# Router logits on GpSimd and VectorE instead of TensorE, in a fused attention and mixture-of-experts kernel

## The reference

```python
x = x + tanh(g_xattn[0]) * cross_attention0(ctx, layernorm(x))   # 8 heads of 64
x = x + tanh(g_ffn[0]) * experts0(layernorm(x))                  # 8 experts, top 2, capacity 40 per batch
x = x + tanh(g_xattn[1]) * linear_attention1(layernorm(x), ctx)
x = x + tanh(g_ffn[1]) * experts1(layernorm(x))

def experts0(x):                        # the part that routes
    probs = softmax(x @ Wr + br)        # Wr is 256 x 8
    topk_p, topk_e = top_k(probs, 2)
    pos = ...                           # how many earlier rows of the batch chose the same expert
    keep = pos < cap
    slot = (topk_e * B + b) * cap + min(pos, cap - 1)
    # rows go to their slots, each expert's two products run over its slots, answers are gathered back
```

## Time and profile before

| | |
|---|---|
| time, median of 3 runs (range) | 2261.21 us (2253.23 to 2261.25) |
| the profiled execution's own time | 2261.54 us |
| its span, first to last instruction | 2259.8 us |
| mean granted TensorE clock | 0.992 of full speed |
| TensorE busy | 2198.2 us (97%) |
| VectorE busy | 1615.2 us (71%) |
| ScalarE busy | 1292.9 us (57%) |
| GpSimd busy | 642.3 us (28%) |

### The profile page before, as it was taken

One profiled execution on the slowest core, in us unless ns is written; L12 is line 12 of the kernel. 1 busy time (PEld: TensorE's weight loads), 2 busy tenths in 40 slices (PEclk: granted clock), 3 DMA queues, 4 the chain that ended last, 5 costly groups with the idle time before them and its releaser, 6 DMA issues. The chain is left out here.

```text
span 2259.8 us, 49398 instructions
## 1 busy us (share of the span) xinstructions
PE 2198.2 (97%) x15486; PEld 1871.1 (83%) x15486; DVE 1615.2 (71%) x5729; ACT 1292.9 (57%) x3251; POOL 642.3 (28%) x1162
## 2 busy tenths in 40 slices
PE   9999999999999999999999999999989999999997
PEld 6777777777777777777689999999978888888886
DVE  5667677677677676777665555555579999999986
ACT  6676776776766767767533343343245555555553
POOL 1123222232232222322320000000255555555541
PEclk9999999999999999999989999999999999999999
DMA  5431111111111111111142222221222222222210
GB/s 195 136 102 45 54 44 47 53 45 47 53 36 53 44 46 54 45 47 38 40 142 72 80 85 84 67 85 47 82 59 65 64 64 63 64 68 64 64 38 19
DMA packets 136226, 146.70 MB, mean 65 GB/s; under 512 B 23090, under 2 KB 122665, under 8 KB 135840
## 3 DMA queue, kind: packets, MB, share of 16 engines
q1 hardware_dynamic: 122825, 122.13, 17.3%
q0 software_dynamic: 12288, 21.21, 3.5%
q10 hardware_dynamic: 855, 0.19, 0.1%
HBM read 101.04 MB, written 54.79 MB: 69 GB/s over the span
## 5 line engine op out<-in xcount | busy, mean ns | idle before, releaser
L735 ACT ACTIVATE a_prob<-a_prob,a_nmax 128x376 f32<-128x376 f32 x512 | 309.8, 607 | 143.8 <-DVE a_nmax L881 143.8
L881 DVE CUSTOM_DVE_ANT_0 a_prob<-a_score,a_mask_row 128x376 f32<-128x376 f32 x512 | 270.4, 543 | 92.3 <-PE a_score L1157 84.6
L1472 ACT ACTIVATE e_hidden<-e_first,keep_b 128x256 f32<-128x256 f32 x320 | 134.4, 472 | 283.0 <-PE e_first L80 282.4
L80 PE MATMUL e_second<-e_w,e_hidden 128*128 128x256 f32 x1920 | 239.5, 284 | 0.0
L80 PEld LDWEIGHTS e_second<-e_w,e_hidden 128*128 128x128 f32 x1920 | 232.6, 192 | 0.0
L1166 PE MATMUL a_turned<-keep_ident,a_prob 128*128 128x128 f32 (+1 forms) x1536 | 216.7, 277 | 1.1 <-DVE a_probT L901 0.7
L1166 PEld LDWEIGHTS a_turned<-keep_ident,a_prob 128*128 128x128 f32 (+1 forms) x1536 | 173.5, 142 | 41.0 <-issue 26.8
L743 ACT ACTIVATE a_probT<-a_turned 128x384 f32<-128x384 f32 x256 | 125.8, 492 | 127.6 <-PE a_turned L1166 127.6
L901 DVE COPY a_probT<-a_turned 128x384 f32<-128x384 f32 x256 | 141.1, 551 | 78.4 <-PE a_turned L1166 75.4
L1157 PE MATMUL a_score<-a_kT,a_qT 64*128 64x376 f32 x1024 | 196.4, 501 | 0.6
L177 POOL TENSOR_SCALAR r_var<-r_mv 128x2 f32<-128x2 f32 x64 | 12.3, 192 | 569.8 <-issue 502.4
(11 more groups left out here) (238 smaller groups left out, 5180.9 us busy)
## 6 DMA issues: line engine op xcount, KB each, us to landing
a_share<-shares SPq DMA_DIRECT2D x256, 64.0 KB, 2.6
w_in<-W SPq DMA_DIRECT2D x32, 512.0 KB, 4.2
slots<-a_zeros SPq DMA_DIRECT2D x8, 1280.0 KB, 8.6
keep_rows<-slots SPq DMA_DIRECT2D x40, 256.0 KB, 4.1
answers<-e_y SPq DMA_DIRECT2D x40, 256.0 KB, 2.2
a_xn<-x SPq DMA_DIRECT2D x32, 256.0 KB, 3.2
a_xr<-x SPq DMA_DIRECT2D x32, 256.0 KB, 3.3
shares<-a_rden_rows SPq DMA_DIRECT2D x512, 0.5 KB
```

Source lines behind the costliest of these rows:

```text
L80: last = nc.tensor.matmul(out, stationary(a, t), moving(b, t), start=start and n == 0, stop=stop and n == len(todo) - 1)
L735: nc.scalar.activation(prob[:, u % 4, a], prob[:, u % 4, a], ACT.Exp, bias=nmax[:, u % 4, a:a + 1], scale=-1.0, accum_out=den[:, u % 4, a: ...
L881: nc.vector.tensor_tensor_reduce(prob[:, u % 4, a], score[SCORE_AT[u][a]][:, 0:NKV], mask_row[:, p], -1.0, 3.0e38, ALU.add, ALU.min, nmax[ ...
L1472: nc.scalar.activation(hidden[:, 2 * j + i], first[:, j, i * CH:(i + 1) * CH], ACT.Relu, bias=b1[:, 2 * j + i, bass.ds(e, 1)]).then_inc(re ...
```

## The change

For batches 0 to 30 the router's logits no longer go through TensorE. The 256 x 8 weights are loaded once more, spread over all 128 partitions (`wr_rows`, in the space of `b2`, row by row, so that the weights of one expert lie 32 bytes apart). GpSimd multiplies the two 256-wide rows of `x2h` of each partition with the weights of expert e, for e from 0 to 7 (`weigh`, 128x512 elements each, into four rotating buffers: two in the second half of `w2_in`, `rT`, and the new `a_weighed`). VectorE sums each product over its 256 columns (`logit_part`), then adds the bias (`logits_sum`). Seven of the eight sums stand at the end of step b+3, the eighth, the bias and the shift at the beginning of step b+4, the choice behind them. `router_exp` moves to that step too.

`router_count` moves down half a step, to where `router_turn` was, and `counts_in` and `place` on VectorE with it. Both halves of `dispatch` are issued in step b+5: the first behind `norm1`, the second behind `norm2` of batch b+2. The waits that kept the banks in order are replaced by ones that fit.

As `w2_in` and `b2` are now in use until the last product, the load of the second half of the first expert's W2 and that of `b2` move from step 4 to step 34. Batch 31 in `experts` keeps the way through TensorE.

```diff
+    wr_rows = keep["b2"][:].rearrange("p e d -> p (e d)").rearrange("p (d e) -> p d e", e=E0)
+    w2_rows = keep["w2_in"][:].rearrange("p k d -> p (k d)")[:, KH * D // 2:].rearrange("p (n k d) -> p n k d", k=QT, d=D)
+    weighed = [w2_rows[:, 0], w2_rows[:, 1], rT[:].rearrange("p k (i d) -> p (k i) d", d=D)]   # a_weighed is appended
...
+    def weigh(eng, b, p, e):
+        if e == 0:
+            eng.wait_ge(x2h_ok, QT * (b + 1))
+            if b == 0:
+                eng.wait_ge(small_in, 16 * N_SMALL)
+        at_least(eng, part_ok, E0 * b + e + 1 - len(weighed))
+        nc.gpsimd.tensor_tensor(weighed[e % len(weighed)], x2h[:, p],
+                                wr_rows[:, :, e].unsqueeze(1).to_broadcast([P, QT, D]), ALU.mult).then_inc(weighed_ok, 1)
+    def logit_part(eng, b, e):
+        eng.wait_ge(weighed_ok, E0 * b + e + 1)
+        nc.vector.reduce_sum(lgr[:, :, e], weighed[e % len(weighed)], AX.X).then_inc(part_ok, 1)
+    def logits_sum(eng, b):
+        eng.wait_ge(part_ok, E0 * (b + 1))
+        nc.vector.tensor_tensor(lg[:], lgr[:], br[:].unsqueeze(1).to_broadcast([P, QT, E0]), ALU.add).then_inc(soft, 1)
...
+                     (r["wr_rows"], t["Wr0"].partition_broadcast(P))]        # one more small load
...
     GpSimd, step s
                 if here(s - 3):
                     norm1(eng, s - 3)
                 if routed(s - 5):
-                    dispatch(eng, s - 5, q, range(QT, QT * 2))
+                    dispatch(eng, s - 5, q, range(QT))
                 if live(s):
                     norm0(s)
                 if here(s - 3):
                     norm2(eng, s - 3)
-                if routed(s - 4):
-                    dispatch(eng, s - 4, p, range(QT))
+                if routed(s - 5):
+                    dispatch(eng, s - 5, q, range(QT, QT * 2))
                 if live(s - 2):
                     residual(s - 2, p)
+                if here(s - 3):
+                    for e in range(E0):
+                        weigh(eng, s - 3, q, e)
...
     ScalarE: router_in(s - 3) goes out, router_exp(s - 3) becomes router_exp(s - 4) behind exps(s - 2, 5, 1)
...
     VectorE, step s, in its new order (unchanged calls in short)
                 attended(s-3, 3); turned_out(s-2, 1, 1)
+                logit_part(eng, s - 4, 7)
                 row_max(s-2, 5, 0); att_low(s-3, 3)
+                logits_sum(eng, s - 4)
                 row_max(s-2, 5, 1)
+                logits_shift(eng, s - 4)
                 mask_line(s-1); over_sum(s-2, 1); kvin_low(s-1, 0)
                 choose 0 to 7 follow, one at a time, up to row_max(s-2, 7, 1)   # before: choose 7 in front of turned_out(s-2, 2, 1)
                 out_norm(s-3); stat(s); turned_out(s-2, 4, 1); x1_stat(s-3)
                 row_max(s-1, 0, 0) ... turned_out(s-2, 6, 1)                    # before: place 0 to 4 in here
+                counts_in(s-4); row_max(s-1, 2, 0); place 0; row_max(s-1, 2, 1); place 1
                 attended(s-2, 2)
+                logit_part 0; place 2
                 turned_out(s-2, 7, 1)
+                logit_part 1; place 3
                 row_max(s-1, 3, 0)
+                logit_part 2; place 4
                 att_low(s-2, 2)
+                logit_part 3
                 row_max(s-1, 3, 1)
+                logit_part 4
                 over_sum(s-1, 0); turned_out(s-1, 0, 1)
+                logit_part 5
                 row_max(s-1, 4, 0)
+                logit_part 6
                 row_max(s-1, 4, 1)
...
     TensorE, step s
-                if routed(s - 4):
-                    eng.wait_ge(v_ok, 3 * (s - 1))
-                    router_count(eng, s - 4, bank_b)                             # between turn_prob 2 and scores 6
...
-                if here(s - 3):
+                if routed(s - 4):
                     if s == B + 1:
                         eng.wait_ge(att_ok, KI * (s - 2) + 1)
                     else:
                         eng.wait_ge(v_ok, 3 * (s - 1) + 1)
-                    router_turn(eng, s - 3, q, bank_b)                           # between turn_prob 6 and scores 2
+                    router_count(eng, s - 4, bank_b)
...
-                    router_logits(eng, s - 3, bank_a)                            # behind times_v 2
...
     SyncE, step B + 2
+                    eng.wait_ge(part_ok, E0 * (B - 1))
+                    load_w2(1)
+                    eng.wait_ge(weighed_ok, E0 * (B - 1))
+                    eng.dma_start(keep["b2"][:], t["b2"].partition_broadcast(P)).then_inc(keep["biases_in"], 16)
```

More of the change, by code:

```diff
@@ L546, in load_w1, with load_w2 @@
                     eng.dma_start(stage_kv[:, n], t["W1"][0, n * P:(n + 1) * P]).then_inc(keep["w1_loaded"], 16)
[L547 to L553, removed]
+                load_w2(0)
+                eng.dma_start(keep["b1"][:], t["b1"]).then_inc(keep["biases_in"], 16)
+            def load_w2(n):
+                half = slice(n * KH // 2, (n + 1) * KH // 2)
+                eng.dma_start(keep["w2_in"][:, half],
+                              t["W2"][0, n * HID // 2:(n + 1) * HID // 2].rearrange("(k p) d -> p k d", p=P)) \
+                    .then_inc(keep["w2_loaded"][n], 16)
             def load_rows(g):
@@ L774, in step @@
                     exps(s - 2, 5, 1)
+                if here(s - 4):
+                    router_exp(eng, s - 4)
+                if live(s - 2):
                     v_out(s - 2, p, 0)
@@ L998, in step @@
                 if here(s - 4):
+                    choose(eng, s - 4, 2)
+                if live(s - 2):
+                    turned_out(s - 2, 2, 1)
+                if here(s - 4):
+                    choose(eng, s - 4, 3)
+                if live(s - 3):
+                    out_centre(s - 3)
+                if live(s - 2):
+                    row_max(s - 2, p, 6, 0)
+                if here(s - 4):
+                    choose(eng, s - 4, 4)
+                if live(s - 2):
+                    row_max(s - 2, p, 6, 1)
+                    over_sum(s - 2, 2)
+                if here(s - 4):
+                    choose(eng, s - 4, 5)
+                if live(s - 2):
+                    attended(s - 2, 0)
+                    turned_out(s - 2, 3, 1)
+                if here(s - 4):
+                    choose(eng, s - 4, 6)
+                if live(s - 2):
+                    row_max(s - 2, p, 7, 0)
+                    att_low(s - 2, 0)
+                if here(s - 4):
                     choose(eng, s - 4, 7)
                 if live(s - 2):
-                    turned_out(s - 2, 2, 1)
-                if live(s - 3):
-                    out_centre(s - 3)
-                if routed(s - 4):
[L1005 to L1013, removed]
                     row_max(s - 2, p, 7, 1)
@@ L1298 @@
 N_FIRST = 5
-N_SMALL = 9
+N_SMALL = 10
 N_CONST = 6
```

103 lines of the change are left out of this document (50 added, 53 removed).

## The result

The changed kernel takes 2475.66 us (median of four runs, 2471.47 to 2476.77) against 2260.88, a ratio of 1.0955 (95% interval 1.0929 to 1.0982). The profiled execution is the one of 2471.47. The forecast had the sign and the place, and half of the size: +102 us were forecast, +215 came.

What follows compares the result with a forecast made beforehand. TensorE's queue set the 34.65 us step before; a closed loop of 36.3 us plus 2.0 of shut-out would make it 38.3, 3.65 slower. 28 x 3.65 = 102 on 2262 gives 2364 us, range 2285 to 2430.

Steps and rivals of the forecast that it cites:

- the loop: Closed chain of queues and waits from one attention output product to the next: 36.3 us a step, 38.3 with the shut-out.
- Output product to the second statistics: First two links, on VectorE: 3.06 us to the product's statistics, then 10.6 to the end of the second statistics.
- a sum per expert: VectorE's 512-element sum of each product out of SBUF: 0.36 to 0.60 us, taken as 0.60.
- count to third attention product: TensorE link from the counting product to the start of the third attention product: 1.66 us.
- The once-only transfers: Extra 1 MB broadcast at the start and later W2 and b2 loads: each 0 to 8.6 us, taken as 0.
- Two of its signs: att_low, like the placing operations, over 1 us at times; TensorE waiting before the output product for att_low.
- shut-out: VectorE's two-SBUF-input operations waiting for GpSimd's products at placing parts 0, 2, 3, 4 and att_low: 2.0 us a step, bound 3.2.
- a clock that falls: Rival, chance 0.08: TensorE's clock drops after standing still, 8.4 us in every third step, giving 2440 us.
- The landing: ScalarE's standardising waits for the moved dispatch's second scatter to land: 3.87 us after the scale and shift.
- the scale and shift: GpSimd link from the end of VectorE's second statistics to the scale and shift: 2.24 us.
- Steps, 30 instead of 28: The per-step loss of 3.65 us was multiplied by 28: 27 full steps and one for the incomplete ones.
- the 1.94: Estimated us per GpSimd product if the 32-byte read step costs half as much again; GpSimd-bound rival, chance 0.12.

Runs made afterwards that it cites:

- fast version: Changed kernel with scatters issued early, placing moved behind the next step's first att_low, and router weights laid out by expert: 2228.26 us, timed 2229.77, ratio 0.987 to the kernel before.
- making products shorter: Changed kernel with the router's weights laid out one expert behind the other, read at 4 bytes instead of 32: 2382.87 us, 93 less.
- short pads: Changed kernel with 7, 6 and 6 dummy TensorE products, shorter than the waits, at three places: 2438.97 us, 37 less.
- early scatters: Changed kernel with all four scatters of a batch issued right behind norm1: 2369.54 us, 106 less.
- late placing: Changed kernel with the five placing parts moved to VectorE's next step, behind the first att_low: 2359.75 us, 116 less.
- the three single edits: Changed kernel with one edit each: scatters behind norm1 (2369.54 us), placing behind the next step's first att_low (2359.75), weights by expert (2382.87).
- placing put back: Changed kernel with early scatters and weights by expert, placing among the products again: 2283.05 us, 55 more than the 2228.26 with placing moved too.

## Why the prediction was half right

Right: the direction, the loop as what sets the step, and most of its links. Output product to the second statistics was forecast with 13.7 us and is 13.4; standardising to value eviction 1.63 against 1.57; a sum per expert advances VectorE by 0.60 us; count to third attention product is 1.61 to 1.68 us wherever the clock holds, against 1.66. ScalarE waits for the scatter and TensorE for the value eviction, at the places named. The once-only transfers cost nothing that shows, as assumed.

Two of its signs did not come. `att_low`, one of the five places of the shut-out, is over 0.6 us in only 2 of 92 records. And TensorE has a single wait for it ahead of the output product in 1,000 us; the wait in its place is ahead of `turn_c`, for ScalarE's second value eviction (39.2 us in 21 steps).

The result lies in the band above 2430 us, which was given 0.08, for a clock that falls on top of the shut-out; both came, but the clock is only one of the terms that were off. Off, in us a step, of the 3.55 between 38.3 and 41.85:

- **The shut-out, +1.6.** Taken as 2.0 with a bound of 3.2, it is 3.6. The step that failed is "after one such wait the next product is mostly over when VectorE comes again". It priced five places with one wait each. But parts 2, 3 and 4 of the placing hold two, two and three operations, and VectorE comes to the second one at once, when GpSimd has already gone on to the next product (713.86 to 713.89). Had I counted operations instead of places, half a product for each of the eight would have made a bound of 5.2 (8 x 1.295 / 2). Taking placing away (-116 us) and putting it back into the fast version (+55) answer to this term; making products shorter (-93) does in part. The link itself, from one `attended` to the last one, is 12.77 us where 9.4 and 2.0 were forecast.
- **The clock, +1.2.** A rival with a chance of 0.08, put aside because "each gap lies between stretches of full work". The clock fell in nearly every step all the same. Its price was estimated as 8.4 us in every third step, 76 us on top of the shut-out (2440); the short pads give back 37 us in all, so that rival comes nearer than the forecast by an overestimate of this term and without the others. It was kept out of the sum as a separate case, but it comes with the waits: the mean clock is 0.947 with all the waits, 0.969 with the early scatters, 0.976 with the late placing and 0.995 with all three edits, and part of the slower work is on the loop.
- **The landing, +0.5, and the scale and shift, +0.3.** The dispatch was timed at 3.87 us behind r_sh and takes 4.41; in the step shown the first scatter starts 0.92 us behind r_sh, where 0.20 was taken from the old place. Of the link, the early scatters take back 3.2.
- **Steps, 30 instead of 28**: 2 x 7.2 = 14 us.

The sum: 28 x 3.6 + 14 = 115 us on the 2364, 2479 against 2475.66. The shut-out alone would have given 2364 + 28 x 1.6 = 2409 us, still inside the range; with the clock it is 2442, outside it. So the two steps that failed are the size of the shut-out and the clock that was left out of the sum.

The product took 1.55 us, between the 1.295 that I used and the 1.94. The Trainium skill, page "GPSIMD Engine Reference", section "Performance pitfalls for Q7 kernels", has half as much again for reads with a step over 8 bytes; here 1.55 against 1.285 us is a fifth more, and the measurement decides. The 0.26 us didn't make GpSimd the bound, but they show in two places, the chain of products and the waits of VectorE; how the 93 us divide between these isn't shown.

What stays open: the shares depend on each other (the three single edits give 106 + 116 + 93 = 315 us, together 247), so the split above is one reading of the links. And of the two operations that wait within a part, the traces show the order of starts and ends, not how the engines' access is granted.

## What to carry to other kernels

Where a loop of waits through several engines sets the step, add up its links; an edit that lengthens one is paid nearly in full, and repairs of different links add up (106 and 116 us became 213) until another bound is met, here nearly TensorE's own work. Work moved to GpSimd in long operations should be kept apart in time from VectorE's short SBUF-to-SBUF operations, and these are counted one by one, not by place. When an idle engine's scatter reads a buffer that is soon written again, its landing belongs at the earliest place in the queue, not behind the next step's scalars.

## What the runs showed of the hardware that I had not expected

- How long an operation stands bears no relation to its size in these rows: a single-input r_kept of 128x4 took 1.52 us, a cast of 128x4 1.24 us in the median with placing put back, while a sum over 512 elements a lane out of SBUF took 0.670 to 0.684 us in 184 records beside the same products. The Trainium skill, page "SBUF — State Buffer", section "Who interferes with whom", has the first two among the kinds that can need the ports shared with GpSimd and the sum among those that never do; the trace agrees with both.
- While VectorE waits, a product is hardly longer (1.65 and 1.55 us beside r_kept and r_slot, 1.52 in the median of all 248), so GpSimd loses more by the late sums (1.17 and 1.10 us in the step shown) than in the product.
- In the step shown TensorE's clock fell not behind the longest wait (2.61 us ahead of the count; the eight score products behind it take 1.53 us, the full rate) but in the second of two shorter ones close together (1.58 and 1.90 us), at 717.6. It stayed at 1.00 for nearly all of the stage when these places were filled, also by pads that were shorter than the waits (6 half-rate stretches in place of 40).
